# Recomputing two spilled pairs in the last pass of a two-convolution block, and loading part of one input early

## The reference, cut to what matters

```
g  = _gn(x)
y1 = conv3x3(g, quantize(w1)) + b1        # first sums
a  = relu(batchnorm(y1))                  # statistics over all images
y2 = conv3x3(a, quantize(w2)) + b2        # second sums
out = x + relu(batchnorm(y2) + g)
```

## Time and profile before

| | us |
|---|---|
| median of 3 runs (lowest, highest) | 535.89 (535.75, 536.9) |
| the profiled execution | 533.88 |
| its span | 532.1 |
| PE busy in it | 481.6 (91%) |
| DVE busy | 416.1 (78%) |
| ACT busy | 344.0 (65%) |
| end of the second convolution, start of the last pass | about 402 to 406 |

### The profile page before, as it was taken

How to read it: one execution, slowest core, us unless ns; L and a number is a source line. 1 busy time by engine, 2 the same in 40 slices (tenths; PEclk the granted TensorE clock), 3 DMA queues, 4 the chain that set the end, 5 groups by cost and what they waited for, 6 DMA issues and landing times.

```text
span 532.1 us, 21191 instructions
## 1 busy us (share of the span) xinstructions
PE 481.6 (91%) x9781; PEld 402.4 (76%) x9781; DVE 416.1 (78%) x613; ACT 344.0 (65%) x390; POOL 94.9 (18%) x153
## 2 busy tenths in 40 slices
PE   3999999999999999999999999999996855988780
PEld 1899999999999787899888989888884432544340
DVE  7999989999999757988988887788877851765550
ACT  3898899998999955765555556665514724764450
POOL 2027366666551500040000000000000000000000
PEclk9999999999999999999999999999998995998996
DMA  8834775433333000044333300000065999999998
GB/s 291 338 129 130 261 263 190 169 127 133 128 136 130 8 7 7 32 171 168 128 129 129 124 4 4 2 4 4 2 245 180 366 407 432 424 427 430 430 428 343
DMA packets 22529, 99.27 MB, mean 187 GB/s; under 512 B 6568, under 2 KB 9000, under 8 KB 17320
## 3 DMA queue, kind: packets, MB, share of 16 engines
q1 hardware_dynamic: 20816, 81.55, 40.4%
q10 hardware_dynamic: 1624, 16.36, 7.3%
HBM read 61.48 MB, written 35.50 MB: 182 GB/s over the span
## 4 chain that ended last, share of the span: by engine, by line
PE 75%; DMA 16%; DVE 4%; ACT 2%; issue 1%; SPq 0%; DVEq 0%
PE conv_ps L1051 71%; DMA split<-in_x_dram 6%; DMA slots<-in_x_dram 5%; DMA xa<-in_x_dram 4%; PE conv_ps L1140 3%; ACT conv_ps L636 1%; DMA out_dram<-split 1%; DVE slots L998 1%; DVE split L1006 1%; DVE slots L1001 1%; PE conv_ps L1014 1%; ACT split L475 0%; DVE gn_tup L727 0%; DVE slots L1006 0%; PE conv_ps L1049 0%
## 5 line engine op out<-in xcount | busy, mean ns | idle before, releaser
L1051 PE MATMUL conv_ps<-split,wmat 64*64 64x385 f16 (+3 forms) x9216 | 380.4, 324 | 1.2 <-ACT split L475 1.2
L1051 PEld LDWEIGHTS conv_ps<-split,wmat 64*64 64x64 bf16 x9216 | 342.8, 107 | 35.2 <-DVE wmat L710 1.4
L509 ACT ACTIVATE slots<-conv_ps,par,evac_scale 128x784 f32<-128x784 f32 x124 | 123.8, 999 | 94.1 <-PE conv_ps L1051 92.3
L1140 PE MATMUL conv_ps<-slots,wmat 128*128 128x392 f32 x224 | 79.7, 515 | 23.4 <-ACT conv_ps L636 23.4
L828 DVE BATCH_NORM_STATS2 bn_tup<-slots 128x6 f32<-128x392 f32 x166 | 81.9, 555 | 15.6 <-ACT slots L509 15.6
L1140 PEld LDWEIGHTS conv_ps<-slots,wmat 128*128 128x128 f32 x224 | 43.7, 198 | 59.5 <-issue 32.3
L727 DVE BATCH_NORM_STATS2 gn_tup<-slots 128x6 f32<-128x448 f32 x112 | 61.8, 612 | 0.9 <-DMA slots<-in_x_dram 0.9
L795 DVE TENSOR_TENSOR split<-slots,split 128x3136 f16<-128x3136 f32 (+4 forms) x36 | 57.2, 1608 | 3.5 <-ACT slots L489 0.9
L797 DVE SCALAR_TENSOR_TENSOR split<-slots,split 128x3248 f16<-128x3248 f32 (+3 forms) x18 | 53.6, 2978 | 2.3
L1006 DVE SCALAR_TENSOR_TENSOR slots<-conv_ps,split 128x784 f32<-128x784 f32 x28 | 27.3, 975 | 30.2 <-PE conv_ps L1140 30.2
L636 ACT ACTIVATE conv_ps<-split,skip_b,skip_s 128x784 f32<-128x784 f32 x28 | 26.9, 996 | 31.7 <-DMA split<-in_x_dram 25.6
(11 more groups left out here) (120 smaller groups left out, 256.8 us busy)
## 6 DMA issues: line engine op xcount, KB each, us to landing
slots<-in_x_dram SPq DMA_DIRECT2D x51, 392.0 KB, 5.4
out_dram<-slots SPq DMA_DIRECT2D x10, 1568.0 KB, 24.6
split<-in_x_dram ACTq DMA_DIRECT2D x5, 1568.0 KB, 15.4
slots<-in_x_dram SPq DMA_DIRECT2D x4, 1568.0 KB, 7.4
y_spill<-slots SPq DMA_DIRECT2D x3, 1624.0 KB, 7.1
slots<-y_spill SPq DMA_DIRECT2D x3, 1624.0 KB, 7.4
y_spill<-slots SPq DMA_DIRECT2D x3, 1568.0 KB, 5.8
split<-in_x_dram SPq DMA_DIRECT2D x3, 1568.0 KB, 8.8
```

The source lines that it names most:

```text
L509: nc.scalar.activation(dst, src, ACT.Identity, bias=bias, scale=scale, accum_out=total).then_inc(evacuated[ph], 1)
L1051: return nc.tensor.matmul(bank[:, r0:r1, w0:w1], lhs, rows[:, top + r0:top + r1, w0 + kx - 1:w1 + kx - 1], start=n == 0 and part is hi_all ...
L1140: mm = nc.tensor.matmul(sums_in(k)[:, h], diag, addend[:, h], start=False, stop=True, skip_group_check=True)
```

## The change

The last pass takes the pairs in another order (`ORDER3`). Of the three pairs whose second sums were spilled, one still is (`RELOADED`, position 15). For the other two (`AGAIN`, positions 7 and 10) the y2 is not stored: both convolutions are computed again from x in the last pass, by ACT (`make_act1`, `make_hi1`, `make_act2`, `seed_again`), DVE (`again_low1`, `again_low2`) and PE (`again_round1`, `again_round2`), and PE adds the skip from the fp16 halves (`add_parts`). While PE is at that, the positions 5, 6, 8 and 9 are computed as position 0 is, on ACT and DVE alone (`TWO_PASS`), each in two halves. The first 1456 columns of the x of position 5 are loaded into the halo columns of the 13 slots (`slots[:, :, PIX:AREA]`, 112 columns each) before the last pass. The x buffers become a list by position (`x3`). All loads are issued by SP. Small tiles are packed in one (`small`), which later holds a diagonal; the other two diagonals go into `bn_tup`.

```diff
-    PAIR3 = [PAIR2[SPILL], PAIR2[NP - 1], *PAIR2[SPILL + 1:NP - 1], *PAIR2[:SPILL]]
-    SLOT3 = [SLOT2[SPILL], None, *SLOT2[SPILL + 1:NP - 1], *SLOT2[SPILL:2 * SPILL]]
+    AGAIN = (7, 10)
+    RELOADED = NP - 1
+    ORDER3 = (SPILL, NP - 1, *range(SPILL + 1, SPILL + 6), 0, SPILL + 6, SPILL + 7, 1, *range(SPILL + 8, NP - 1), 2)
+    assert sorted(ORDER3) == list(range(NP))
+    PAIR3 = [PAIR2[t] for t in ORDER3]
+    SLOT3 = [None if u == IN_PSUM or u in AGAIN else SLOT2[ORDER3[5 if u == RELOADED else u]] for u in range(NP)]
     FREE = SLOT2[NP - 1]
+    TWO_PASS = (0, 5, 6, 8, 9)
+    RING = [u for u in range(NP) if u not in TWO_PASS]
...
+    STORES = [PARTS0, 2, 2, 2, 1, 2, 2, 2, 2, 2, 2, 1, 1, 1, 2, 4]
+    STRIP = AREA - PIX
+    EARLY = RES * STRIP
+    IN_STRIPS = 5
+    CUTS2 = {u: (0, EARLY if u == IN_STRIPS else PIX // 2, PIX) for u in TWO_PASS}
...
+
+        halves = [split[:, k].rearrange("p h a -> p (h a)").bitcast(F32) for k in range(2)]
+        x3 = [ap[:, 0:PIX] for ap in (
+            slots[:, FREE], halves[0], halves[1], xa, slots[:, FREE], xa, slot3(2), slot3(0), xa, slot3(2), slots[:, FREE],
+            halves[0], halves[1], xa, slot3(2), slot3(0))]
+        again1 = [ap.bitcast(F16)[:, 0:2 * PIX].rearrange("p (h m) -> p h m", h=2) for ap in (halves[0], slot3(3))]
+        again_fp32 = [ap[:, 0:PIX] for ap in (halves[1], slot3(4))]
+        again2 = [ap.bitcast(F16).rearrange("p (h m) -> p h m", h=2) for ap in (halves[1], slot3(4))]
...
+            sp.dma_start(slots[:, :, PIX:AREA], strips(pair_view(x, PAIR3[IN_STRIPS])[:, 0:EARLY])).then_inc(strips_loaded, 16)
...
+            store_first()
+            store_ring(1)
+            wait_stored(0)
+            load(7)
+            store_ring(2)
+            store_ring(3)
+            wait_out(3)
+            load(5)
+            wait_stored(2)
+            load(6)
+            store_ring(4)
+            wait_out(4)
+            load(10)
+            store_two_pass(5)
+            wait_out(5)
+            load(8)
+            store_two_pass(6)
+            wait_out(6)
+            load(9)
+            wait_stored(5)
+            sp.wait_ge(y2_spilled, 16)
+            sp.dma_start(slot3(RELOADED)[:, 0:PIX], y2_spill).then_inc(y2_loaded, 16)
+            store_ring(7)
+            wait_out(7)
+            load(11)
+            load(12)
+            store_two_pass(8)
+            wait_out(8)
+            load(13)
+            store_two_pass(9)
+            wait_out(9)
+            load(14)
+            wait_stored(7)
+            load(15)
+            for u in range(10, NP):
+                store_ring(u)
...
+            def make_act1(r):
+
+                bias, scale = again_affine(r)
+                sc.wait_ge(again_coef, len(AGAIN))
+                sc.wait_ge(x3_loaded[AGAIN[r]], 16)
+                if r == 0:
+                    sc.wait_ge(ring_out, nth(2, NQ - 1))
                 else:
-                    sc.wait_ge(out_ready, FIRST[u - 1] + k + 1)
-                    i = PAIR3[u]
-                    src, bias, scale = banked(x3_buffers[u % 4], u, k), skip_b[:, i:i + 1], skip_s[:, i:i + 1]
-                nc.scalar.activation(sums_in(k), src, ACT.Identity, bias=bias, scale=scale).then_inc(seeded, 1)
+                    sc.wait_ge(stored[4], 16 * STORES[4])
+                nc.scalar.activation(again_fp32[r], x3[AGAIN[r]], ACT.Identity, bias=bias, scale=scale).then_inc(again_act1, 1)
+
+            def make_hi1(r):
+                bias, scale = again_affine(r)
+                u = (IN_PSUM, 3)[r]
+                sc.wait_ge(stored[u], 16 * STORES[u])
+                nc.scalar.activation(again1[r][:, 0], x3[AGAIN[r]], ACT.Identity, bias=bias, scale=scale).then_inc(again_hi1, 1)
+
+            def make_act2(r, q):
+
+                sc.wait_ge(again_coef, len(AGAIN) + 2)
+                if q == 0:
+                    sc.wait_ge(again_lo1, r + 1)
+                if (r, q) == (1, 0):
+                    sc.wait_ge(two_out, first_two(IN_STRIPS) + 1)
+                sc.wait_ge(again_conv1, NQ * r + q + 1)
+                src = again_sums1(q)
+                nc.scalar.activation(again_rows2(again2[r][:, 0], q), src, ACT.Relu, bias=again_w[:, 1:2],
+                                     scale=again_w[:, 0:1]).then_inc(again_hi2, 1)
+                nc.scalar.activation(src, src, ACT.Identity, bias=again_w[:, 1:2], scale=again_w[:, 0:1]).then_inc(again_act2, 1)
+
+            def seed_again(r, q):
+                sc.wait_ge(again_coef, len(AGAIN) + 3)
+                sc.wait_ge(again_conv2, NQ * r + q + 1)
+                nc.scalar.activation(sums_in(q), sums_in(q), ACT.Identity, bias=again_w[:, 2:3],
...
+            seed_last(3)
+            for u in (2, 3):
                 for k in range(NQ):
-                    if k == NQ - 1 and 6 <= u + 3 < NP:
-                        sc.wait_ge(out_ready, FIRST[u])
-                        sc.dma_start(x3_buffers[(u + 3) % 4], pair_view(x, PAIR3[u + 3])).then_inc(x3_loaded[(u + 3) % 4], 16)
+                    seed(u, k)
+            make_act1(0)
+            seed(4, 0)
+            seed(4, 1)
+            make_hi1(0)
+            seed(4, 2)
+            seed(4, 3)
+            two_affine(5, 0)
+            two_affine(5, 1)
+            make_act2(0, 0)
+            two_affine(6, 0)
+            make_act2(0, 1)
+            two_affine(6, 1)
+            make_act2(0, 2)
+            make_act2(0, 3)
+            seed_again(0, 0)
+            make_act1(1)
+            seed_again(0, 1)
+            make_hi1(1)
+            seed_again(0, 2)
+            two_affine(8, 0)
+            seed_again(0, 3)
+            two_affine(8, 1)
+            make_act2(1, 0)
+            two_affine(9, 0)
+            make_act2(1, 1)
+            two_affine(9, 1)
+            make_act2(1, 2)
+            make_act2(1, 3)
+            for q in range(NQ):
+                seed_again(1, q)
+            for u in range(11, NP):
+                for k in range(NQ):
...
+            def two_pass(u, step):
+                k = step // 2
+                n = first_two(u) + k + 1
+                if (u, step) == (IN_STRIPS, 0):
+                    dve.wait_ge(strips_loaded, 16)
+                elif step == (2 if u == IN_STRIPS else 0):
+                    dve.wait_ge(x3_loaded[u], 16)
+                if step % 2 == 0:
+                    sum_and_add(u, half_of(u, k), two_affine_ready, n - PARTS0)
+                else:
+                    relu_and_add(u, half_of(u, k), n)
+
+            def finish(u, k):
+                dve.wait_ge(skip_added, nth(u, k))
+                nc.vector.scalar_tensor_tensor(out=banked(out_of(u), u, k), in0=sums_in(k), scalar=0.0, in1=banked(x3[u], u, k),
+                                               op0=ALU.max, op1=ALU.add).then_inc(ring_out, 1)
+
+            def again_low1(r):
+                dve.wait_ge(again_act1, r + 1)
+                dve.wait_ge(again_hi1, r + 1)
+                nc.vector.tensor_tensor(again1[r][:, 1], again_fp32[r], again1[r][:, 0], ALU.subtract).then_inc(again_lo1, 1)
+
+            def again_low2(r, q):
+                dve.wait_ge(again_hi2, NQ * r + q + 1)
+                dve.wait_ge(again_act2, NQ * r + q + 1)
+                nc.vector.scalar_tensor_tensor(out=again_rows2(again2[r][:, 1], q), in0=again_sums1(q), scalar=0.0,
+                                               in1=again_rows2(again2[r][:, 0], q), op0=ALU.max,
...
+            dve.wait_ge(x3_loaded[4], 16 * PARTS0)
+            finish(4, 0)
+            finish(4, 1)
+            again_low1(0)
+            finish(4, 2)
+            finish(4, 3)
+            for r in range(2):
+                u = (5, 8)[r]
+                for q in range(NQ):
+                    two_pass(u, q)
+                    again_low2(r, q)
+                for q in range(NQ):
+                    two_pass(u + 1, q)
+                    finish(AGAIN[r], q)
+                    if (r, q) == (0, 1):
+                        again_low1(1)
+            for u in range(11, NP):
+                dve.wait_ge(x3_loaded[u], 16)
+                for k in range(NQ):
+                    finish(u, k)
 
...
+            def again_round1(r, q):
+                pe.wait_ge(again_hi1, r + 1)
+                pe.wait_ge(ring_out, nth((4, AGAIN[0])[r], q))
+                for part in range(2):
+                    if part == 1:
+                        pe.wait_ge(again_lo1, r + 1)
+                    for n in range(9):
+                        for a in range(2):
+                            for b in range(2):
+                                mm = again_tile1(r, q, part, n, a, b, n == 8 and part == 1)
+                mm.then_inc(again_conv1, 1)
+
+            def again_round2(r, q):
+                pe.wait_ge(again_lo2, NQ * r + q + 1)
+                for part in range(2):
+                    pe.wait_ge((again_hi2, again_lo2)[part], NQ * r + min(q + 2, NQ))
+                    for n in range(9):
```

(41 more changed lines are left out.)

334 lines of the change are left out of this document (225 added, 109 removed).

## The result

| | before | after |
|---|---|---|
| median of four runs each, measured together (us) | 536.08 | 549.3 (548.24 to 550.82) |
| the profiled execution | 533.88 | 549.96 |
| its span | 532.1 | 548.2 |

The changed kernel takes 1.0246 times as long (95% interval 1.0217 to 1.0276), 13.2 us by the medians and 16.1 by the spans (the profiled execution of before is 2.2 us under its median, that of after 0.7 above). The forecast was 541.1 us, a loss of 5.2, with a range of 534.5 to 549. The direction is right and the size is not. (In what follows one execution of e4, at 1074.8 us, is left out as disturbed.)

What follows compares the result with a forecast made beforehand. The last pass was taken as bound by DMA bytes. Pair 6's end at 471.4, plus 1.0, 61.9, 0.3 and 2.7, gave span 537.3, 5.2 over 532.1; added to the 535.89 median: 541.1 us, range 534.5 to 549.

Steps and rivals of the forecast that it cites:

- What is taken away, and the cost outside the last pass: Last pass loses two reloads and 0.464 of a load, 9.2 us with DMA full; work added before it costs nothing.
- Step 1: Last pass: load(7), which waits for store 0, is issued at 420.2 and lands at 428 us.
- Step 2: Last pass: after load(7) ACT does act1, two seeds of pair 4 and hi1, ending at 435.9 us.
- Step 3: Last pass: PE's clock drops after standing still; pair 4's first two quarters take 2.4 us, not 1.32, ending near 437.9.
- Step 4: Last pass: from 437.9 DVE has 30.4 us of work and 3.1 of waits, ending pair 6 at 471.4.
- Step 5: After pair 6: 1.0 us to first data, 61.9 for 16.5 units at 428 GB/s, 0.3 for shorter runs, 2.7 tail.
- The slack of 8 to 11 us behind pair 6: Last pass after pair 6: each store is ready 8 to 11 us before the queue reaches it, so waits cost nothing.
- The prediction's other sum, by idle time: Last pass: 9.2 us of bytes saved, 16 us of emptied queue added, some 1.6 less for pair 1's longer runs.
- DMA stays full: Rival, last pass: the queue never empties and the saved bytes give 526.7 us; 6 in 100.
- DVE without waits: Rival, last pass: DVE reaches pair 6's end without waiting, time 536 to 538 us; 12 in 100.
- The clock stays down on PE: Rival, last pass: recomputed rounds run at half clock, 6 us instead of 3.0, time 547 to 553; 12 in 100.
- The rate falls: Rival, long full stretch: 369 GB/s instead of 428, so 16.5 units take 71.8 us, time 551; 3 in 100.

Runs made afterwards that it cites:

- e4: The changed kernel without the early strips, so all of load(5) is in the last pass: 549.19 us, 1.0259 of before.
- e5: The kernel before with 20 stores of 1.6 MB to a scratch tensor added under its second convolution: 556.59 us, 1.04 of before.
- e3: The changed kernel with only 2 of 9 taps in the recomputed convolutions: 543.67 us, 1.0164 of before.
- e1: The changed kernel with the reload, first half of store 7 and load(12) issued ahead of store 6's second half: 547.31 us, 1.0223 of before.
- e8: The changed kernel with one pair recomputed, not two, loads and reloads issued earlier, and 100 matmuls added to keep PE's clock up: 534.14 us, 0.997 of before.
- e9: The kernel before with ACT's ten loads issued by SP instead: 536.36 us, 1.0016 of before.

## Why the prediction was right in direction and wrong in size

The forecast for the span was 537.3; it was 548.2. The mechanism was right in the main: SP's queue in order runs dry while DVE and PE recompute, and that costs more than the bytes saved. Three terms of the sum failed: the landing of load(7), which came 3.4 us late even from its own issue; the waits of DVE for PE up to the end of pair 6, 7.5 us instead of 3.1; and the rate behind it, 410 GB/s instead of 428. The 10.9 us stand in these steps:

- **What is taken away, and the cost outside the last pass.** Right but for an offset: the kernel after is 1.2 us later in its first convolution already (the last evacuation at L622 begins at 206.10, the one before at 204.89), and load(1) goes out at 402.62 instead of 401.41. I had priced nothing there; its cause wasn't tested. 0.6 us of it are left when load(7) is issued.
- **Step 1, load(7).** Issued at 420.82 (forecast 420.2), landed at 432.0 (forecast 428). This is the term that was mis-sized most, by 3.4 us, and not by chance of one run: seven others with this load gave 9.5 to 10.7 us from issue to landing, where I had 7.8. The bytes in front were right: by the windows from 408 on, 3.4 MB had gone at the issue, so 1.4 of the 4.8 MB issued stood in front, and with the load's own 1.6 that is 3.0 MB. At the rates of the windows from 420 (413, 339 and 362 GB/s) these had gone at 428.9, 0.7 us more than at my rates. The rest is the landing, for which I took 0.5. Each of the 16 engines adds one to the load's semaphore when its part has landed, and the trace has these 16 times: thirteen lie between 429.3 and 430.0, the others at 430.7, 430.8 and 432.0. ACT waits for all 16, so the slowest engine sets the time: 1.0 us to the mean of the parts and 2.1 more to the last. In the eight runs the mean part landed 8.8 to 9.1 us after the issue and the last one 0.5 to 2.1 behind it. I had priced no such straggler. Why one engine lags was not tested.
- **Step 2, ACT.** Right: from the landing to the end of hi1 7.8 us, forecast 7.9.
- **Step 3, the clock.** Right in the rows: 0.50 from 436 to 440, and low1 began 10.3 us after the landing, forecast 9.9.
- **Step 4, DVE to the end of pair 6.** 36.6 us instead of 33.5. DVE is busy 29.1 of them (forecast 30.4) and waits 7.5, where I had 3.1; the waits in front of two finishes are 5.4 alone. Two causes: instruction fetches that come late under a full queue (2.4 us of PE here, the mechanism of e5), which no step or rival of mine had; and a first round of 3.9 us (PE on it from 444.0 to 447.9, with its halo rows at L1433), where I took 3.0. With the convolutions cut (e3) 4.4 us go. And the forecast saw too much room here: the 5.7 us that it has for DVE "per round", in the rival on the clock, are what two rounds take (both passes of a half, 3.7, and two low2, 2.0). Per round DVE has 2.8 us of work, less than PE's 3.0, so PE's rounds could hold DVE up at full clock already: the first three low2 began 3.4 us apart (450.11, 453.48, 456.85).
- **Step 5, the rest.** The amount is right: 26.4 MB moved after 480, which is 16.5 units. They took 64.5 us, not 61.9 plus 0.3, at 410 GB/s instead of 428; some windows are far below, as 488 to 492 (297 GB/s at share 0.97). Reckoned back as in the forecast, the data began 1.4 us after pair 6's end instead of 1.0 (the first packet itself starts after 0.9), and the tail was 3.3 instead of 2.7.
- **The slack of 8 to 11 us behind pair 6.** Wrong: 5.6 us by the sum under e1, where a queue fed earlier runs dry again before the second half of store 9. By the same sum this wait costs nothing in the kernel after.

In sum: 0.6 for the start, 3.4 for load(7), 0.4 up to low1, 3.1 for DVE's stretch, 0.4 for the first data, 2.3 for the rate and 0.6 for the tail, 10.8 of the 10.9.

The prediction's other sum, by idle time (9.2 us of bytes saved, 16 of emptied queue, 1.6 gained in longer runs), can be laid beside the whole pass, from 408 us to the span's end (before, then after):

```profile
408.00:532.10 124.10, 86.92 (x240) 47.34 (x240) 65.39 (x69) 60.32 (x63) 0.00 (x0) 0.88 0.98 402
408.00:548.20 140.20, 110.12 (x1496) 74.14 (x1496) 92.04 (x80) 85.37 (x77) 1.58 (x3) 0.92 0.85 329
```

Without the rounding of the shares the queue is empty for 3.0 and 21.5 us: 18.5 us were added, where the forecast has 16. The bytes, 49.8 and 46.1 MB, are as forecast and worth 9.1 us. But while it is busy the queue moves 388 GB/s instead of 411, which costs 6.6 us where the forecast had a gain of 1.6. Seen like this the rate is the larger part of what was missed. Some of it is hidden in the sum by steps: where the queue runs dry afterwards, a slower transfer only makes the hole shorter.

**The rivals.** *DMA stays full* is refuted by the two holes of 3.4 and 8.3 us. *DVE without waits* is refuted by the 2.98 and 2.40 us. *The clock stays down on PE* gave 547 to 553, and the time came out there, but by other means: the clock was 1.00 from 444 on. *The rate falls*, which got 3 in 100, is part of the truth: not at 369 throughout, but 410 over the stretch. The Trainium skill, DMA: Bandwidth & Descriptors, section Bandwidth, has two figures for transfers between HBM and SBUF: about 358 GB/s as the share of one core when both cores of the pair stream, and 425 GB/s measured for a load of 16 MB with the other core idle. This kernel runs on one core, so the second was the one to lay beside it, and the traces agree: 418 GB/s for loads alone, 426 for loads and stores in the slice at 493 us. The prediction quoted the first without its condition and was right not to use it. The stretches at 297 to 305 are below both, so neither figure marks them. *The strips* harm nothing.

**What would show it.** The holes at 440 and 464 to 472 came at 444 and 469 to 480; at 454 there is no empty queue but loads at 304 GB/s. The second half of store 6 was due at 471 to 472 and went at 479. DVE waited 7.5 us in its stretch, where it should have had hardly any idle time. And the prediction's own sign against it came: the rate of the long full stretch was 410 GB/s, not 420 to 430.

## What to carry to other kernels

A byte saved in a pass that is bound by transfers is worth nothing if the engines' new work lets the queue run dry; ask of every wait on the issuing queue which independent transfers stand behind it, and after moving them look for the next such wait. Price work that is added to PE under a full data queue with its code: an unrolled convolution fetches it all the time, and each late fetch here cost 0.3 to 3 us. Price a load up to the landing on the slowest of its 16 engines, here up to 2.1 us behind the mean. And try the half of such a change: one recomputed pair, with its queue kept fed, gained 0.3% where two lost 2.5%.

## What the runs showed of the hardware that was not expected

- Fetches of instructions compete with data. 20 stores that nobody waits for, under a convolution that PE ran without a gap, made it stand still nine times for 0.26 to 2.57 us and cost 21.2 us. PE resumed 2.1 to 2.6 us after the start of the instruction queue's packet, in all nine; one packet of ten came without a stop.
- In some stretches the queue moves about 300 GB/s with its 16 engines busy (304 at 452, 297 at 488 us in the kernel after; 286 at 452 in e8), where long stretches before ran at 428 and loads alone at 418. The packets themselves take longer there: those of 12,544 bytes 658 ns from 452 to 456 and 712 from 488 to 492, against 470 in the kernel before from 500 to 520. That all transfers go through one queue is not the cause (e9), nor is a convolution on PE beside stores alone: under the stores of e5 it stayed at 412 to 426. Loads beside a convolution were not tried by themselves. The cause was not found.
- The 16 engines that share one DMA drift apart in a full queue. Load(7) landed on thirteen of them within 0.7 us and on the last 2.0 us later, and the stores issued behind it landed in the order of issue with similar stragglers. Over 1 MB of those stores had moved before load(7) counted as landed. That looks like a later transfer overtaking an earlier one, but the landing times need no overtaking, only the late engines.
